# Last pass of a graph network: positive part taken in the division, mean's sum taken from the skip addition

## The reference, cut to what matters

```
h = (x @ W).reshape(N, 4, 64)
e = leaky_relu(a_src[src] + a_dst[dst]);  e = exp(e - segment_max(e)[dst])
denom = segment_sum(e, dst);  alpha = e / denom[dst]
out = segment_sum(h[src] * alpha, dst).reshape(N, 256) + bias
out = relu(out)
norm = sqrt(sum(out * out, axis=-1))
out = out / maximum(norm, 1e-12)
x = layernorm(x + out)          # (v - mean(v)) / sqrt(var(v) + 1e-5)
```

## Time and profile before

| | |
|---|---|
| median of 3 runs | 6150.03 us (6143.17 to 6152.39) |
| profiled execution | 6138.69 us, span 6136.9 us |
| PE busy | 5167.8 us (84%) |
| DVE busy | 4560.9 us (74%) |
| ACT busy | 3817.9 us (62%) |
| POOL busy | 3041.7 us (50%) |

### The profile page before, as it was taken

One profiled execution on the slowest core, in us unless ns is written; L12 is line 12 of the kernel. 1 busy time (PEld: TensorE's weight loads), 2 busy tenths in 40 slices (PEclk: granted clock), 3 DMA queues, 4 the chain that ended last, 5 costly groups with the idle time before them and its releaser, 6 DMA issues. The chain is left out here.

```text
span 6136.9 us, 94789 instructions
## 1 busy us (share of the span) xinstructions
PE 5167.8 (84%) x23690; PEld 3888.2 (63%) x23690; DVE 4560.9 (74%) x13038; ACT 3817.9 (62%) x11901; POOL 3041.7 (50%) x2581
## 2 busy tenths in 40 slices
PE   2788899999999988888888998988899989945654
PEld 1566666666677776767666666667777767733443
DVE  7676655555677787887787888878878777768886
ACT  0587765666899766666655555565555567755555
POOL 1677777422444455555355665543333230057776
PEclk7899999999999999999988888889999989955555
DMA  1577543343566554545344444434544431134442
GB/s 49 183 266 255 193 136 113 125 142 112 195 221 220 184 183 165 190 171 183 137 141 155 157 154 159 161 109 141 166 153 152 137 109 54 39 115 138 139 138 94
DMA packets 362734, 925.74 MB, mean 151 GB/s; under 512 B 66872, under 2 KB 140715, under 8 KB 362198
## 3 DMA queue, kind: packets, MB, share of 16 engines
q1 hardware_dynamic: 271078, 702.73, 33.4%
q0 software_dynamic: 91120, 216.96, 12.1%
HBM read 568.39 MB, written 361.72 MB: 152 GB/s over the span
## 5 line engine op out<-in xcount | busy, mean ns | idle before, releaser
L2207 POOL DMA_INDIRECT got<-hop,end_i x600 | 642.6, 1071 | 725.0 <-PE psum L1014 466.0
L2207 POOL DMA_INDIRECT got<-tab,end_i x600 | 702.8, 1171 | 441.7 <-PE psum L1122 266.7
L1122 PE MATMUL psum<-got,sf 128*128 128x264 f32 (+2 forms) x1200 | 470.4, 482 | 365.0 <-DVE got L1946 288.4
L1014 PE MATMUL psum<-got,sf 128*128 128x256 f32 x1600 | 507.1, 399 | 104.8 <-ACT got L1278 96.8
L1122 PEld LDWEIGHTS psum<-got,sf 128*128 128x128 f32 x1200 | 238.8, 240 | 470.6 <-DVE got L1946 350.4
L1014 PEld LDWEIGHTS psum<-got,sf 128*128 128x128 f32 x1600 | 289.5, 195 | 269.4 <-issue 99.8
L2298 POOL DMA_INDIRECT out<-res,out_i x200 | 211.4, 1057 | 463.9 <-DMA out<-hd 358.0
L963 PE MATMUL psum<-h_t,w 128*128 128x512 f32 x784 | 380.3, 616 | 68.5 <-DVE h_t L1705 68.5
L1162 ACT ACTIVATE squares<-res,l_sv 128x256 f32<-128x256 f32 x600 | 297.3, 496 | 223.7 <-DVE l_sv L1851 188.7
L1278 ACT COPY got<-psum 1x256 f32<-1x256 f32 x796 | 280.0, 352 | 239.2 <-PE psum L1014 184.2
L1316 ACT ACTIVATE res<-res,l_mo 128x256 f32<-128x256 f32 x600 | 310.8, 589 | 147.7 <-DVE l_mo L1839 147.5
(11 more groups left out here) (438 smaller groups left out, 14914.2 us busy)
## 6 DMA issues: line engine op xcount, KB each, us to landing
own<-hop SPq DMA_DIRECT2D x150, 512.0 KB
x_t<-res SPq DMA_DIRECT2D x150, 512.0 KB
xo<-x_t SPq DMA_DIRECT2D x150, 512.0 KB, 3.7
hop<-res SPq DMA_DIRECT2D x100, 512.0 KB
x_in<-in_x SPq DMA_DIRECT2D x98, 512.0 KB, 4.6
out<-hd SPq DMA_DIRECT2D x98, 512.0 KB
tab<-tab SPq DMA_DIRECT2D x50, 536.0 KB, 2.7
own<-tab SPq DMA_DIRECT2D x50, 536.0 KB
```

The lines of the kernel that those rows point to most:

```text
L1014: T.matmul(o, sf_of(q)[:, k * P:(k + 1) * P], got_of(q)[:, k * FEAT:(k + 1) * FEAT], start=(p < 3), stop=True).then_inc(at("l_agg"), 1)
L1122: T.matmul(bank(3 + k % 2)[:, 0:g.ext], sf_[:, k * P:(k + 1) * P], got_of(q)[:, k * g.width:k * g.width + g.ext], start=True, stop=True).t ...
L2207: eng.indirect_dma_start(out=dst, out_offset=None, in_=table, in_offset=bass.IndirectOffsetOnAxis(ap=idx, axis=0), bounds_check=rows_ - 1, ...
```

## The change

In p = 6, the division is four instructions (one for each chunk), which take the maximum of the sum and zero before they multiply. The part `rlu` is gone, and `sqr` waits for the division itself. The row sum for the mean no longer comes from `rlu`; the four additions of `u` write out their accumulators, and behind a wait for them one small operation makes the negative mean from them. For p = 4 and 5 the division is as before. In `schedule`, five lengths of p = 6 are other than before, and the part `rlu` is not there.

```diff
-                put(("V", "vals", q), 2.0 if p == HOPS else 0.8, here("Sexp", "Ggather"))
+                put(("V", "vals", q), {4: 2.0, 5: 0.8, 6: 1.45}[p], here("Sexp", "Ggather"))
                 me = "Gmine" if p == HOPS else "Vmine"
-                put((me[0], "mine", q), 3.1 if p == HOPS else 0.75, here("Sexp", "Yown"))
+                put((me[0], "mine", q), 3.1 if p == HOPS else 1.3 if p == 6 else 0.75, here("Sexp", "Yown"))
...
-                put(("V", "merge", q), {4: 3.2, 5: 1.0, 6: 1.7}[p], here("Vagg3") + ...
+                put(("V", "merge", q), {4: 3.2, 5: 1.0, 6: 2.1}[p], here("Vagg3") + ...
             if p == 6:
-                put(("S", "rlu", q), 1.75, here("Vmerge") + [("V", "u", q - 2)] * (i >= 2))
-                put(("S", "sqr", q), 1.75, here("Srlu") + [("V", "sn", q - 2)] * (i >= 2))
+                put(("S", "sqr", q), 2.4, here("Vmerge") + [("V", "sn", q - 2)] * (i >= 2))
...
-                put(("V", "u", q), 1.8, here("Grn", "Yxo") + [("S", "sqv", q - 2)] * (i >= 2))
+                put(("V", "u", q), 2.3, here("Grn", "Yxo") + [("S", "sqv", q - 2)] * (i >= 2))
...
-            elif name == "rlu":
+            elif name == "sqr":
                 eng.wait_ge(at("g_o"), q - HOPS * ng + 1)
-                if i >= 2:
-                    eng.wait_ge(at("g_u"), i - 1)
-                for k in range(K):
-                    m = S.activation(res_of(q)[:, k, :], res_of(q)[:, k, :], ACT.Relu, accum_out=l_sv[:, par, 0, k:k + 1])
-                m.then_inc(at("g_relu"), 1)
-            elif name == "sqr":
-                eng.wait_ge(at("g_relu"), i + 1)
...
-                m = V.tensor_tensor(o, sums, by(den[:, par, 1, 0:hk]).unsqueeze(3).to_broadcast([P, K, g.heads, g.cols]), ALU.mult)
-                m.then_inc(at("g_o"), 1)
+                inverse = by(den[:, par, 1, 0:hk]).unsqueeze(3).to_broadcast([P, K, g.heads, g.cols])
+                if p == 6:
+                    for k in range(K):
+                        m = V.scalar_tensor_tensor(o[:, k], sums[:, k], 0.0, inverse[:, k], ALU.max, ALU.mult)
+                    m.then_inc(at("g_o"), 1)
+                else:
+                    V.tensor_tensor(o, sums, inverse, ALU.mult).then_inc(at("g_o"), 1)
...
-                V.scalar_tensor_tensor(l_sv[:, par, 1, :], l_sv[:, par, 0, :], -1.0 / (16 * FEAT), l_ss[:, par, 2, :], ALU.mult, ALU.mult)
                 for k in range(K):
-                    m = V.scalar_tensor_tensor(res_of(q)[:, k, :], res_of(q)[:, k, :], l_ss[:, par, 2, k:k + 1], xo_of(q)[:, k, :], ALU.mult, ALU.add)
-                m.then_inc(at("g_u"), 1)
+                    m = V.scalar_tensor_tensor(res_of(q)[:, k, :], res_of(q)[:, k, :], l_ss[:, par, 2, k:k + 1], xo_of(q)[:, k, :], ALU.mult, ALU.add,
+                                               accum_out=l_sv[:, par, 0, k:k + 1])
+                m.then_inc(at("g_us"), 1)
+                eng.wait_ge(at("g_us"), i + 1)
+                V.tensor_scalar(l_sv[:, par, 1, :], l_sv[:, par, 0, :], -1.0 / (16 * FEAT), None, ALU.mult).then_inc(at("g_u"), 1)
```

More of the change, by code:

```diff
@@ L419, in schedule @@
                 free_ = room if p != 5 else ([("T", "tz", q - 2)] if i >= 2 else [])
-                put(("V", "merge", q), {4: 3.2, 5: 1.0, 6: 1.7}[p], here("Vagg3") + ([("S", "sqv", q - 2)] if p == 4 else []) + free_ + (here("Yxo") if p == 4 else []) + early("V", "merge", 1))
+                put(("V", "merge", q), {4: 3.2, 5: 1.0, 6: 2.1}[p], here("Vagg3") + ([("S", "sqv", q - 2)] if p == 4 else []) + free_ + (here("Yxo") if p == 4 else []) + early("V", "merge", 1))
             if p == 6:
-                put(("S", "rlu", q), 1.75, here("Vmerge") + [("V", "u", q - 2)] * (i >= 2))
-                put(("S", "sqr", q), 1.75, here("Srlu") + [("V", "sn", q - 2)] * (i >= 2))
+                put(("S", "sqr", q), 2.4, here("Vmerge") + [("V", "sn", q - 2)] * (i >= 2))
                 put(("V", "sn", q), 0.2, here("Ssqr") + [("V", "u", q - 2)] * (i >= 2))
                 put(("G", "rn", q), 1.05, here("Vsn"))
-                put(("V", "u", q), 1.8, here("Grn", "Yxo") + [("S", "sqv", q - 2)] * (i >= 2))
+                put(("V", "u", q), 2.3, here("Grn", "Yxo") + [("S", "sqv", q - 2)] * (i >= 2))
                 put(("S", "sqv", q), 2.1, here("Vu") + [("V", "sv", q - 2)] * (i >= 2))
```

## The result

The change made the kernel slower: 6208.19 us (6201.99 to 6214.64) against 6147.73 us, a ratio of 1.0098 with a 95% interval of 1.0081 to 1.0116. Run once more in another set, the changed kernel took 6210.9 us against 6154.57, a ratio of 1.0097 (1.0069 to 1.0124). The profiled execution's span is 6200.3 us, 63.4 us over that of before.

What follows compares the result with a forecast made beforehand. VectorE's fixed order in the last pass, with TensorE at half clock, was taken as the bound. +20 - 19 - 14 - 2 = -15 us on the profiled 6138.69 gave 6124, as median 6135 us; range 6080 to 6205.

Steps and rivals of the forecast that it cites:

- The bound and the frame: Last pass alone, TensorE at half clock: VectorE's fixed order sets 15.28 us a group; the change counts in 47 groups.
- The division: Division on VectorE in the last pass: four instructions in place of one cost +0.22 us a group.
- The half-rate rival: Each of the four division pieces on VectorE takes 0.345 us longer, +83 us in all, 6233 us; chance 0.02.
- `u`: Additions on VectorE in the last pass: accumulators and a second wait, less L2139, cost +0.20 us a group.
- The price of the work: Added VectorE work of division and `u` in the last pass: +0.42 us a group, 47 groups, +20 us.
- ScalarE's and GpSimd's waits: VectorE's waits for ScalarE and GpSimd in the last pass lose 0.4 of 0.57 us a group, -19 us.
- TensorE's waits: VectorE's waits for TensorE in the last pass, 1.56 us a group, fall by a fifth, 0.3 us, -14 us.
- The tail: Behind the last division, `rlu` leaves the chain: 1.6 us go, counted as -2 us.
- The bounds: All VectorE waits in the last pass: from -1.43 us a group (GpSimd's 13.85) to about +1.5 (TensorE waits double).
- the new order lets VectorE run into TensorE: VectorE reaches L1946, L1975 and L2056 earlier against plan and waits one microsecond more a group: +65, 6215 us; chance 0.13.

Runs made afterwards that it cites:

- the order by hand: Changed kernel's instructions with each engine's order of the last pass written out by hand from group 4 on; 6080.35 us, ratio 0.9879 to the kernel before.

## Why the prediction was wrong

The forecast was 6135 us, faster; the kernel is at 6208, just over the range. By its steps:

- *The bound and the frame* held: TensorE at half clock in the last pass, the dense work's end unmoved (the first division behind it starts at 5409.36 us, 5408.94 before), nothing lost ahead of it. The whole of it lies in the 47 groups: from the first to the last of their divisions 765.3 us in place of 697.5.
- *The division*, +0.22 us: measured 1.43 to 1.50 us for the four against 1.23, so +0.20 to +0.27. Right. The half-rate rival is out: the mean length is 425 ns, where half rate would need about 690.
- *`u`*, +0.20 us: from the first addition at 5730.54 to the next instruction's start at 5732.33 are 1.79 us, against 1.67 with L2139. So +0.12; the accumulator reads lie under their neighbours as in the earlier trace rows. The price of the work, +0.42, was really +0.3 to +0.4. (Its ends, given as +0.2 and +0.9, add up to +0.30 and +0.84.) VectorE's busy time in a group, forecast at 13.0, grew by only 0.13 us, since small operations ran about 0.2 us a group shorter: L2070's 225 ns are 165 in L2062, L2061's 235 are 192 in L2053, L2132's 208 are 165 in L2130. Why isn't shown.
- *ScalarE's and GpSimd's waits*, -0.4 of 0.57 us: this step failed. ScalarE's did go, 0.29 to 0. GpSimd's went from 0.28 to 1.85 us. I had argued from the chain (ScalarE is done earlier, so what follows is) and not from the queue in which the powers stand. The chain's head start is worth nothing to a power that stands behind a gather or a store in its queue, when the gather waits for the end of an aggregation. So the term of -19 us was really 47 x 1.28 = +60 us, about all of the loss.
- *TensorE's waits*, -0.3 us: measured +0.12. The argument that long pieces, known as such, would each be put over a matmul did not hold. With the old lengths and without `rlu` in the plan these waits are about 2.2, with those that name no engine counted.
- *The tail*, -2 us: from the last division's start to the span's end are 25.6 us after and 30.5 before, so -4.9. That is more than `rlu`'s 1.6, and the rest is order again: before, the last inverse norm's power starts 3.9 us behind its input, as it stands behind four stores; after, it starts at once, and the layer norm's stands 2.2 us behind stores.
- *The bounds*: for what an order can do to the waits I took -1.43 to +1.5 us a group. The new order stands at +1.46, the one by hand at a period of 14.0 near the lower end, 13.85. The lower bound had a ground, GpSimd's time, and the order by hand runs into it. The upper one came out by luck: it was a doubling of the waits for TensorE, and what grew are those for GpSimd. For the likeliest value between the bounds there was no ground.
- *The rivals*: "the new order lets VectorE run into TensorE" gave 6215 us, 7 us from the time, but its mechanism is in the rows only in part. VectorE does come to `sh` early against plan, by 0.25 us of the 2.05 that are missing there, and TensorE's half clock does count, by way of the gather that waits for it. But the place and the engine are others: the waits for TensorE, at L1946, L1975 and L2056 before, grew by 0.12 us in all, and `sh` and `u` wait for GpSimd. That the number is so near is luck.

The new lengths aren't right either. Three are longer than their pieces are now: `sqr` 2.4 for 1.7 us, the division with its inverse 2.1 for 2.0, `u` 2.3 for 1.8. Which of the five tips the order wasn't tried alone.

## What to carry to other kernels

Where a planner's lengths write the order, a change of lengths is a change of order, and it can be worth more than the work that is changed (here +0.6 to +0.8% against +0.1 to +0.4%). Time the two apart: new work in the old order, and old work in the new one. Read waits for a tiny instruction by the queue that it stands in, not by its inputs; what stands ahead of it may wait for something else altogether. And in a stage that repeats, an order written by hand, with a long piece over each wait, can beat the planner's: here a ratio of 0.988 against 0.999 to 1.010 for its four orders.

## What the runs showed of the hardware

A power of 128x4 on GpSimd takes 1.0 us or up to twice as long (1.00 to 2.13 us in the last pass of the kernel before), it seems by what VectorE does meanwhile. In the hand order it stands beside `vals` and `mine`, both with two inputs in SBUF (GpSimd, then VectorE):

```profile
5703.34 1.62 POOL L2276 TENSOR_TENSOR l_mo<-l_mo,power 128x4 f32<-128x4 f32 x1
5704.95 1.65 POOL L2284 TENSOR_TENSOR l_ss<-l_ss,power 128x4 f32<-128x4 f32 x1
```

```profile
5702.83 1.23 DVE L2078 TENSOR_TENSOR got<-got,pp 128x1040 f32<-128x1040 f32 x1
...
5704.51 1.22 DVE L2084 TENSOR_TENSOR own<-own,pp 128x1040 f32<-128x1040 f32 x1
```

The first power ends 0.90 us behind the end of `vals` at 5704.06, the second 0.87 us behind that of `mine` at 5705.73, nearly as if each began only there. The Trainium skill (SBUF — State Buffer, section "Who interferes with whom") says that a VectorE instruction with two SBUF inputs contends with a GpSimd instruction that reads SBUF; the rows agree. The mean of the powers is 1.65 us here, 1.04 in the changed kernel, and as GpSimd is the bound of the hand order, an estimated 1.2 us a group (twice 0.6) may lie in it. That wasn't tried. What the Trainium skill says of `scalar_tensor_tensor` with two float32 sources (Vector Engine (DVE) Microarchitecture Reference, section "Points that are easy to get wrong"), weighed in the prediction, doesn't hold for this form: the four divisions take 425 ns each on the mean, 1.43 to 1.50 us together, and the one of the same 1024 columns with `tensor_tensor` took 1.23.
